# Interleaving two projections in the preparation of a graph-attention kernel, and moving small loads to another DMA queue

## What is computed

```python
n = layernorm(x)                              # x: 6250 x 256
x_l = n @ W_l + b_l                           # left rows
x_r = n @ W_r + b_r                           # right rows
g = leaky_relu(x_r[dst] + x_l[src], 0.2)      # 100000 edges, sorted by dst
alpha = einsum('ehc,hc->eh', g, att) + log(edge_weight)[:, None]
a = softmax of alpha over the edges of each dst
x = x + segment_sum(x_l[src] * a, dst) + bias
x = x + experts(layernorm(x))                 # 2 of 8 experts
```

## Time and profile before

| what | us |
|---|---|
| median of 3 runs | 1822.94 |
| lowest, highest | 1822.12, 1826.45 |
| the profiled execution | 1823.75 |
| its span in the trace | 1822.0 |
| TensorE matmul busy | 1701.7 (93%) |
| VectorE busy | 1404.0 (77%) |
| ScalarE busy | 1259.1 (69%) |
| GpSimd busy | 1247.0 (68%) |

### The profile page before, as it was taken

One profiled execution on the slowest core, in us unless ns is written; L12 is line 12 of the kernel. 1 busy time (PEld: TensorE's weight loads), 2 busy tenths in 40 slices (PEclk: granted clock), 3 DMA queues, 4 the chain that ended last, 5 costly groups with the idle time before them and its releaser, 6 DMA issues. The chain is left out here.

```text
span 1822.0 us, 33908 instructions
## 1 busy us (share of the span) xinstructions
PE 1701.7 (93%) x8561; PEld 1290.9 (71%) x8562; DVE 1404.0 (77%) x2644; ACT 1259.1 (69%) x3162; POOL 1247.0 (68%) x1295
## 2 busy tenths in 40 slices
PE   6886799999999999999999999998797899999998
PEld 4663466666666666666666666665596799999998
DVE  6554899999999999999999999999869433333333
ACT  4722699999999999999989998997770233333332
POOL 1447677777777777777777777776526677766775
PEclk9998999999999999999999999998857999999999
DMA  6588878887878888878778887873764344444444
GB/s 211 120 234 280 250 238 245 243 242 239 237 239 243 240 246 237 241 237 242 241 238 241 240 241 234 242 246 108 231 235 150 79 78 69 69 69 70 71 72 53
DMA packets 208384, 352.59 MB, mean 194 GB/s; under 512 B 43978, under 2 KB 97524, under 8 KB 208101
## 3 DMA queue, kind: packets, MB, share of 16 engines
q0 software_dynamic: 63072, 147.92, 34.0%
q1 hardware_dynamic: 144037, 201.90, 33.9%
q10 hardware_dynamic: 1120, 1.05, 0.2%
HBM read 302.77 MB, written 47.98 MB: 193 GB/s over the span
## 5 line engine op out<-in xcount | busy, mean ns | idle before, releaser
L775 POOL DMA_INDIRECT rows<-left_rows,srcs x880 | 843.2, 958 | 272.5 <-issue 257.0
L1327 PEld LDWEIGHTS p_gain<-W,hots 128*128 128x128 f32 x1760 | 328.1, 191 | 228.7 <-issue 153.2
L1327 PE MATMUL p_gain<-W,hots 128*128 128x264 f32 x1760 | 471.4, 392 | 11.5 <-DVE acc L1101 9.9
L1265 PE MATMUL p_row<-rows,ident 128*128 128x512 f32 x880 | 459.9, 606 | 19.5 <-DMA rows<-left_rows,srcs 19.1
L1781 ACT ACTIVATE e_hT<-e_ph,b_column 128x128 f32<-128x128 f32 x420 | 119.7, 368 | 326.1 <-PE e_ph L1806 326.1
L1152 ACT ACTIVATE L<-p_row 128x512 f32<-128x512 f32 x440 | 261.2, 594 | 92.1 <-PE p_row L1265 88.6
L1222 ACT ACTIVATE far<-iota_row,dl 128x128 f32<-128x128 f32 x880 | 298.8, 390 | 0.0
L1257 PE MATMUL p_row<-rights,hotT 128*128 128x256 f32 x1760 | 280.0, 301 | 17.8 <-DMA rights<-right_rows 11.8
L981 DVE TENSOR_TENSOR L<-L,p_weights 128x1024 f32<-128x1024 f32 x220 | 266.0, 1209 | 11.5 <-ACT L L1152 11.2
L996 DVE TENSOR_REDUCE raw<-L 128x32 f32<-128x1056 f32 x220 | 272.8, 1240 | 1.4 <-issue 0.2
L1072 DVE TENSOR_TENSOR W<-rows,p_weights 128x1024 f32<-128x1024 f32 x220 | 266.3, 1210 | 5.3 <-PE p_gain L1327 1.1
(11 more groups left out here) (259 smaller groups left out, 1820.5 us busy)
## 6 DMA issues: line engine op xcount, KB each, us to landing
rights<-right_rows SPq DMA_DIRECT2D x440, 256.0 KB
locals<-item_locals SPq DMA_DIRECT2D x110, 256.0 KB, 4.0
rows<-left_rows,srcs POOLq DMA_INDIRECT x880
right_rows<-p_parts SPq DMA_DIRECT2D x49, 256.0 KB, 3.4
w<-in_L_ffn_W SPq DMA_DIRECT2D x16, 512.0 KB, 6.3
X<-in_x SPq DMA_DIRECT2D x8, 896.0 KB, 5.0
left_rows<-p_y SPq DMA_DIRECT2D x49, 132.0 KB, 1.8
normed_rows<-acc SPq DMA_DIRECT2D x7, 896.0 KB, 4.5
```

Source lines behind the costliest of these rows:

```text
L775: nc.gpsimd.indirect_dma_start(out=s["rows"][:, g % RINGS, n, :], out_offset=None, in_=d["left"][:, :], in_offset=bass.IndirectOffsetOnAxi ...
L1265: nc.tensor.matmul(p_row[:, n, :].rearrange("p (m f) -> p m f", f=D), s["ident"][:, :], rows[:, g.slot(RINGS), PAIR * n:PAIR * (n + 1), 0: ...
L1327: last = nc.tensor.matmul(p_gain[:, n, 0:D + H], hots[:, g.slot(2), i, :], W[:, g.slot(2), i, :, :].rearrange("p h c -> p (h c)"), start=( ...
```

## The change

A right tile r = t - 7 now follows left tile t for t from 7 to 48, on every engine: `WITH_RIGHT` lists these t, `RIGHT_AFTER` gives r, and `RIGHTS_FIRST` = 42 right tiles are done when the left loop ends. The PSUM slots go round over this mixed order (`place`, `slot_of`). The last 7 right tiles follow. The reads of the edge lists, which stood in one run of 21 on GpSimd, now come two at a time from tile 16 on, with GpSimd's low parts between. The sources, destinations and weights are turned from left tiles 22, 31 and 42 (30, 41 and right tile 12 before); the work on weights, keys and marks moves into the left loop. The store of `item_node_tile` and the small strided loads move from SyncE's queue to ScalarE's. The 24 early gathers stand behind the whole left loop.

```diff
-SRC_TURN, LOCAL_TURN, WEIGHT_TURN = 30, 41, 12
+SRC_TURN, LOCAL_TURN, WEIGHT_TURN = 22, 31, 42
+WITH_RIGHT = [t for t in range(7, NODE_TILES) if True]
+RIGHT_AFTER = {t: r for r, t in enumerate(WITH_RIGHT)}
+RIGHTS_FIRST = len(WITH_RIGHT)
...
+        order = [(side, i) for t in range(NODE_TILES) for side, i in ((0, t), (1, RIGHT_AFTER.get(t, -1))) if i >= 0]
+        order += [(1, r) for r in range(RIGHTS_FIRST, NODE_TILES)]
+        place = {product: i for i, product in enumerate(order)}
...
+                for t in range(NODE_TILES):
+                    if t == ITEMS_READ:
+                        pool.wait_ge(items_done, 1)
+                    if t >= ITEMS_READ:
+                        for i in range(2 * (t - ITEMS_READ), min(3 * QI, 2 * (t + 1 - ITEMS_READ))):
+                            read_rows(i)
...
+                    if RIGHT_AFTER.get(t, 0) % 2:
+                        take_low(RIGHT_AFTER[t])
+                pool.wait_ge(turned_copied, QI)
+                for k in range(4):
+                    pool.wait_ge(left_stored[k], 16 * len(range(k, NODE_TILES, 4)))
+                early = iter(range(EARLY_GROUPS * G))
+                for t in range(RIGHTS_FIRST, NODE_TILES):
+                    if t % 2:
+                        take_low(t)
+                    gather(next(early))
+                for i in early:
                     gather(i)
...
                 for t in range(NODE_TILES):
                     sp.wait_ge(*left_copied(t))
                     sp.dma_start(d["left"][t * P:(t + 1) * P, :], y[:, t % 4, :]).then_inc(left_stored[t % 4], 16)
...
+                    if t in RIGHT_AFTER:
+                        store_right(RIGHT_AFTER[t])
...
                     project_left(t)
+                    if t in RIGHT_AFTER:
+                        pe.wait_ge(operands_done, 2)
+                        project_right(RIGHT_AFTER[t])
...
+                    if t == ITEMS_READ:
+                        act.wait_ge(items_done, 1)
+                        act.dma_start(d["node_tile"].rearrange("(q p) o -> p (q o)", p=P), j_idx[:, :],
+                                      allow_slow_non_contiguous=True).then_inc(stored, 16)
+                    if t == LOCAL_TURN + 9:
+                        act.wait_ge(stored, 16 * 6)
...
-                    if t == 1:
+                    if t == WEIGHT_TURN - 7:
                         v.wait_ge(weight_in, 16 * QI)
```

More of the change, by code:

```diff
@@ L337, in read_rows @@
                     ).then_inc(landed, 16)
[L339 to L343, removed]
                 def gather(i):
@@ L350, in gather, with take_low @@
                     gather_item(nc, d, s, g, n)
-                for t in range(1, NODE_TILES, 2):
+                def take_low(t):
                     pool.wait_ge(right_by_scalar, (t + 1) // 2)
@@ L357, in _ @@
                                             ).then_inc(low_by_pool, 1)
[L358 to L364, removed]
+                for t in range(NODE_TILES):
[4 more added lines that the diff above has]
+                            read_rows(i)
+                    if t == LOCAL_TURN + 2:
+                        pool.wait_ge(local_done, 1)
+                        nc.gpsimd.tensor_copy(local16[:, :, :], local[:, :, :]).then_inc(local_kept, 1)
+                    if RIGHT_AFTER.get(t, 0) % 2:
[9 more added lines that the diff above has]
+                for i in early:
                     gather(i)
@@ L385, in _, with store_right, store_marks @@
                     sp.dma_start(d["right"][NODE_TILES * P:NT * P, side * D:(side + 1) * D], X[:, NODE_TILES, :]).then_inc(stored, 16)
-                flat_keys = d["key"].rearrange("e o -> (e o)")
+                def store_right(t):
+                    sp.wait_ge(*low_of(t))
+                    sp.dma_start(d["right"][t * P:(t + 1) * P, :], parts[:, t % 4, :, :].rearrange("p a f -> p (a f)")
+                                 ).then_inc(right_stored[t % 4], 16)
+                def store_marks(kind):
+                    sp.wait_ge(breaks_done, kind + 1)
+                    sp.dma_start(d["marks"][kind * QI * P:(kind + 1) * QI * P, :].rearrange("(q p) e -> p q e", p=P),
+                                 marks[:, kind, :, :]).then_inc(stored, 16)
                 for t in range(NODE_TILES):
@@ L416, in _ @@
[L416 to L430, removed]
+                for t in range(RIGHTS_FIRST, NODE_TILES):
+                    store_right(t)
+                    if t - NODE_TILES in (-7, -5, -3):
+                        store_marks((-7, -5, -3).index(t - NODE_TILES))
@@ L514, in _ @@
                         turn_back(QI + t - LOCAL_TURN, local)
-                pe.wait_ge(operands_done, 2)
-                for t in range(NODE_TILES):
-                    project_right(t)
                     if WEIGHT_TURN <= t < WEIGHT_TURN + QI:
@@ L521, in _ @@
                         turn_back(2 * QI + t - WEIGHT_TURN, rows_w)
+                for t in range(RIGHTS_FIRST, NODE_TILES):
+                    project_right(t)
             @block.scalar
@@ L552, in copy_back, with copy_right @@
                     nc.scalar.activation(table[:, (i % QI) * P:(i % QI + 1) * P], ps[:, i % 2, 0:P], ACT.Copy).then_inc(turned_copied, 1)
+                def copy_right(t):
+                    act.wait_ge(right_projected, t + 1)
+                    wait(act, low_by_pool, (t - 4 + 1) // 2)
+                    nc.scalar.activation(right[:, t % 4, :], py[:, slot_of(1, t), 0:D], ACT.Copy).then_inc(right_by_scalar, 1)
                 root(0)
@@ L741, in _ @@
                         nc.vector.tensor_scalar(key[:, :, :], key[:, :, :], -1.0, None, ALU.add).then_inc(local_done, 1)
-                for t in range(NODE_TILES):
-                    take_high(t)
-                    take_low(t)
-                    if t == 1:
+                    if t == WEIGHT_TURN - 7:
                         v.wait_ge(weight_in, 16 * QI)
@@ L769, in _ @@
                         last.then_inc(breaks_done, 1)
+                for t in range(RIGHTS_FIRST, NODE_TILES):
+                    take_high(t)
+                    take_low(t)
 def gather_item(nc, d, s, g, n):
```

102 lines of the change are left out of this document (53 added, 49 removed).

## The result

The change takes 1829.21 us (median of 7 runs, 1828.28 to 1834.3) where the kernel before takes 1824.15 beside it (7 runs, 1822.12 to 1828.56): a ratio of 1.0028, 95% interval 1.0015 to 1.0042, so 0.28% slower. On a second chip it was 1827.06 against 1823.36 (1.0020, 1.0008 to 1.0032).

A forecast was written before the change was run, and what follows sets the result against it. The prediction took a fixed-length train of GpSimd gathers behind prepare's barrier as the bound. Stalls of 6 + 4 + 3 = 13 us less 7.6 won move the barrier by +5.4 us, giving 1828.5 us, range 1819 to 1839.

The forecast's parts named there:

- my own case: Whole kernel: stalls of 11 to 18 us give 1826.3 to 1833.3 us; chance 0.36.
- the bound of 0.3%: Whole kernel: 5.5 us is the least a measurement can tell; slower than that 0.47, within it 0.42, faster 0.11.
- one for one: End of prepare: the total time moves exactly as its barrier moves, since a gather train of fixed length, 1087 us, follows.
- the sign that I had set: Edges stage: a gather train shorter than 1087 us by several us would show the one for one rule wrong.
- TensorE's floor: Left loop: mixed rounds of 1.97 us from 30.8 us on; without a stall the loop ends at 120.8 us.
- The tail: After the left loop: gathers start at 122.4 us, barrier at 154.7 without stalls, 7.6 us before the old 162.3.
- GpSimd's reads: Tiles 16 to 26: 31.9 us of reads and low parts against TensorE's 20.7; stall 6 us, bounds 0 and 11.
- The store of `item_node_tile`: Left loop: small writes hold up other queues too, but in the rounds of GpSimd's reads; 0 counted, upper bound 3 us.
- VectorE, 4 us: Tile 35, with statistics, keys and weights in one round, and tiles 7 and 21: stall 4 us, bounds 0 and 7.
- ScalarE, 3 us: Tiles 38 to 44: table load, logarithm and issues add 8.9 us in seven rounds; stall 3 us, bounds 0 and 8.9.
- the wait for keys and locals: ScalarE at tile 40: four rounds, 7.9 us, cover the landing of these stores unless GpSimd holds back SyncE; nothing counted.
- What the profile would show: Prepare and edges: first gather near 135 us, 24th near 168, TensorE idle over 20 us before the barrier, train 1087 us.

The follow-up runs named there:

- second look: The changed kernel, unedited, profiled again beside the kernel before on a second chip: 1827.06 against 1823.36 us; the profiled execution took 1824.77 us.
- run 8: Kernel before, with item_node_tile stored in pieces of 28 bytes and nothing else changed: 1815.12 against 1823.36 us, ratio 0.9957.
- run 12: Changed kernel with 28-byte store pieces, sources' cast two tiles later, spread reads, ScalarE's small loads at tiles 43, 45 and 46: 1817.75 us against 1823.77 for kernel before.
- run 6: Changed kernel with a right tile only behind every odd left tile from the seventh on: 1825.82 us, ratio 1.0014 to the kernel before.
- run 2: Changed kernel with item_node_tile stored as 128 pieces of 28 bytes instead of 896 of 4: 2190.11 us on a slow chip, ratio 1.001 to kernel before.
- run 9: Changed kernel with item_node_tile in 28-byte pieces, once more, again on a slow chip: 2254.22 us against 2244.51 for the kernel before, ratio 1.0052.
- run 10: Changed kernel with 28-byte store pieces, sources' cast at tile 23, GpSimd's reads one a tile from the eighth: 2236.33 us, slow chip, ratio 1.0001 to kernel before.
- run 1: Changed kernel with the store of item_node_tile back on SyncE's queue: 2194.97 us on a slow chip against 2188.62 for the kernel before, ratio 1.0011.
- run 3: Changed kernel with ScalarE's small loads issued on SyncE's queue instead: 2196.41 us on a slow chip, ratio 1.0028 to the kernel before.
- run 4: Changed kernel with VectorE taking high and low parts of every right tile, none on GpSimd or ScalarE: 2210.43 us, slow chip, ratio 1.0099 to kernel before.
- run 11: Changed kernel with right tiles behind odd left tiles only, 28-byte store pieces, cast at tile 23: 2236.79 us on a slow chip, ratio 0.997 to kernel before.

## Why the prediction held, and where it was wrong

The forecast was 1828.5 us, the median 1829.21, within my own case (1826.3 to 1833.3), and just inside the bound of 0.3%; I had thought it a little more likely past it (0.47 against 0.42). By steps:

- **The rule "one for one".** Held only to within 6 us: K's memset moved by +10.3, +5.2, -9.1 and -1.7 us in the change, its second look, run 8 and run 12, and the spans by +10.5, +1.0, -10.7 and -7.7. The train behind isn't quite of fixed length: from K's memset to the end it took 1659.0 us in the change's profile, 1658.8 before, but 1654.7 and 1652.8 in the second look and run 12. Nearly all of that is the train of gathers, 1087.3 us before, 1087.0 in the change, but 1081.5 and 1082.0 in these two; waits for a ring slot were 11.2 and 8.8 us in them, for 13.5 before. By the sign that I had set (a train shorter by several us) the rule fails there. There is one trace of the kernel before, so whether the change or the single execution shortens the train is open. What moves is the 24th gather's end where GpSimd is last, and the barrier where the right tiles are (run 6).
- **TensorE's floor.** Right: mixed rounds are 1.97 us, the first ones at 30.6, 32.5, 34.5; the search adds 3.28 and 1.75.
- **The tail.** From the first gather's start to the 24th's it took 30.8 us, for my 32.3. The term that failed is "its copy and its store's landing take 2.5": the last left product starts at 134.91 us and the first gather at 141.76. By my working (1.1 for the product, 2.5 behind it) this is 3.6 us, measured 6.8, and 6.8 in the second look. The trace shows why. SyncE issues left store 48 only after right store 40, whose low part it awaits, and it lands among right stores. I had this order in the code and priced the landing by an undisturbed store. With 1.5 us gained at the gathers, the tail was 1.7 us longer.
- **TensorE's clock, which the sum doesn't have.** I put no price on it. Behind a standstill TensorE's own instructions took up to twice as long (3.81 for 1.92 us, at 0.50): some 3 of the 7.1 us at tiles 20 to 23, and 3 of the 6.1 at 40 to 43, in the first profile. The kernel before shows the same at 62 to 66 us, so it could have been read there.
- **GpSimd's reads, 6 us.** Right in size (7.1 in the first profile, 7.0 in the second, clock included), wrong in cause. GpSimd was not late: it was itself busy for only 1.1 of the 4 us from 62 to 66, waiting for VectorE. The stores were late, by the small writes, and behind them the sources' cast. Right was that all this falls in the same rounds, and that a queue of its own doesn't shield.
- **The store of `item_node_tile`, nothing of its own.** For the change this is not settled: runs 2 and 9 gain nothing, but on slow chips and with unexplained waits in its place, and the collapse of the traffic opens the stall in both profiles. Runs 10 and 12 show how little is left in these rounds, 0.5 us in run 12, when all three are gone. The section "Issuing engines are not separate DMA queues" of the Trainium skill (DMA: Bandwidth & Descriptors) is borne out by runs 1 and 3: the small writes hold up the tile stores from either queue. In the kernel before the same store was worth 8.2 us, the largest single price in this study, and I passed over it, since the change left it in.
- **VectorE, 4 us.** 2.0 at tile 37 in both profiles, and 0.4 to 0.6 at odd places: 2.5 in all. A little too much.
- **ScalarE, 3 us.** 6.1 in the first profile and 3.0 in the second; the clock is the difference. The step that failed is "nothing" for the wait for keys and locals: it is 2.5 us of standing, and moving the loads by three tiles (run 12) took nearly the whole stall away (0.6 us left at tiles 40 to 45).
- **What the profile would show.** First gather near 135: 141.8 and 136.7. 24th near 168: 172.6 and 167.4. The train 1087 us: 1087.0 and 1081.5. TensorE idle for over 20 us before the barrier: 15.4, since the barrier fell at 158.7 and not behind the gathers. That was wrong: I took "GpSimd has issued its gathers" and "they have run" for one moment.

The stalls sum to 15.8 us in the first profile and 12.6 in the second, for my 13. The good number is in part luck: a tail too short, GpSimd blamed for others, VectorE too dear, the clock left out. K's memset came 10.3 and 5.2 us later for my 5.4, while the medians moved by 5.1 and 3.7.

## What to carry to other kernels

Look at DMA share beside GB/s: a stretch with a high share and almost no bytes was a store in tiny pieces here, and it stopped every engine that waited for any store. Make the pieces longer before you move such a store to another queue. Where several waits end in the same rounds, removing one may show nothing (runs 2 and 9); remove them together, then take them back one by one, which was not done here. When loads are moved forward, move them no further than their data: ScalarE's 2.5 us of standing for a landing cost this kernel more than 8.9 us of its own work spread over seven rounds. Count what stands behind a wait too: TensorE came out of most of its long ones at half its clock.

## What the runs showed that I had not expected

- 896 writes of 4 bytes held all queues for about 8 us (16 to 55 GB/s at a DMA share of 0.8 to 1.3), and 128 writes of 28 bytes for nothing that the windows show (155 to 199 GB/s at 0.53 to 0.62): 8.2 us of the kernel before.
- The other engines pass a barrier while GpSimd's gathers ahead of it still run: at 158.7 us, with K's memset at 173.5.
- While GpSimd issues its reads there are long unexplained waits of ScalarE and VectorE: 22.7 and 17.1 us in run 4, 14.3 in run 3, 13.9 in run 11, 6.4 in run 9, 5.5 in run 2, all on the two slower chips; none in run 1, on one of them. Only 2.8 us was seen on a usual chip (second look), and none in run 8, where 21 reads run back to back too. With reads one a tile there was 0.9 us on a slow chip (run 10) and none on a usual one (run 12). Whether the chip, the length of the loop's code or the queues decide this is open and was not tried by itself.
